# Layer 3's expert FFN: a second activation on ScalarE in place of VectorE's rounding, eight buffers for its results, and weight splits on GpSimd that wait for the normalized x

## What is computed

```python
# x = x + _L3_ffn_ref(_layernorm(x), ...)
shared = silu(x @ sh_up_w + sh_up_b) @ sh_down_w + sh_down_b
scores = softmax(xf @ gate_w.T)
topk_w, topk_i = top_k(scores, 2)
topk_w = topk_w / (topk_w.sum(axis=-1, keepdims=True) + 1e-20)
comb = (one_hot(topk_i, 8) * topk_w[..., None]).sum(axis=1)
h = silu(einsum('nd,edh->neh', xf, up_w) + up_b)
ye = einsum('neh,ehd->ned', h, down_w) + down_b
y = einsum('ned,ne->nd', ye, comb)
return y + shared
```

## Time and profile before

| | us |
|---|---|
| Median of 3 executions | 1869.22 (1867.02 to 1870.14) |
| The profiled execution | 1872.72 |
| its span, from the first to the last instruction | 1870.9 |
| TensorE matmuls busy | 1740.7 (93%) |
| VectorE busy | 1412.7 (76%) |
| ScalarE busy | 1020.7 (55%) |
| GpSimd busy | 640.1 (34%) |

### The profile page before, as it was taken

One profiled execution on the slowest core, in us unless ns is written; L12 is line 12 of the kernel. 1 busy time (PEld: TensorE's weight loads), 2 busy tenths in 40 slices (PEclk: granted clock), 3 DMA queues, 4 the chain that ended last, 5 costly groups with the idle time before them and its releaser, 6 DMA issues. The chain is left out here.

```text
span 1870.9 us, 30938 instructions
## 1 busy us (share of the span) xinstructions
PE 1740.7 (93%) x11311; PEld 1533.4 (82%) x11311; DVE 1412.7 (76%) x3118; ACT 1020.7 (55%) x2239; POOL 640.1 (34%) x906
## 2 busy tenths in 40 slices
PE   6878999999999999999878999999979999999698
PEld 6657899999989999999856888888757788888487
DVE  6467787877878786878676677768877788887786
ACT  3355546555556556555555565656633777776321
POOL 0613030211203030302101455555831666666342
PEclk9989999999999999999999999999989999998799
DMA  5110000000000000000021112110000000000111
GB/s 174 38 48 26 1 7 6 1 12 1 12 1 13 1 12 1 15 1 1 1 91 52 58 56 65 49 68 13 10 1 17 16 18 15 10 10 4 37 54 33
DMA packets 17751, 49.04 MB, mean 26 GB/s; under 512 B 2617, under 2 KB 7362, under 8 KB 15938
## 3 DMA queue, kind: packets, MB, share of 16 engines
q1 hardware_dynamic: 16738, 46.25, 7.6%
q10 hardware_dynamic: 864, 0.83, 0.1%
HBM read 46.15 MB, written 0.92 MB: 25 GB/s over the span
## 5 line engine op out<-in xcount | busy, mean ns | idle before, releaser
L1381 ACT ACTIVATE a_pH<-banks 125x512 fp32r<-125x512 f32 (+1 forms) x384 | 203.9, 544 | 267.6 <-PE banks L195 191.1
L1452 DVE TENSOR_TENSOR a_pL<-banks,a_pH 125x512 fp32r<-125x512 f32 (+1 forms) x384 | 235.4, 623 | 116.6 <-ACT a_pH L1381 114.7
L2011 POOL TENSOR_TENSOR a_prob<-a_prob,a_rinv 112x750 f32<-112x750 f32 x128 | 184.1, 1438 | 196.2 <-DVE a_rinv L2334 196.2
L1433 DVE TENSOR_SCALAR_CACHE_REDUCE a_prob<-banks 128x500 f32<-128x500 f32 x336 | 221.8, 677 | 5.0 <-PE banks L195 4.1
L1225 POOL TENSOR_TENSOR a_head_oH<-a_o,ones 128x256 fp32r<-128x256 f32 (+1 forms) x24 | 16.5, 686 | 605.2 <-DVE a_o L1460 605.2
L1271 PE MATMUL banks<-ident,a_prob 128*125 128x128 f32 x1344 | 201.2, 274 | 6.6 <-ACT a_prob L1366 4.4
L1366 ACT ACTIVATE a_prob<-a_prob,a_nmax 128x1000 f32<-128x1000 f32 x168 | 187.9, 1121 | 32.9 <-DVE a_nmax L1436 32.9
L195 PE MATMUL banks<-a_pH,a_head_vH 125*128 125x256 f32 (+1 forms) x576 | 200.1, 347 | 5.2 <-DVE a_pL L1452 4.3
L1271 PEld LDWEIGHTS banks<-ident,a_prob 128*125 128x125 f32 x1344 | 186.3, 188 | 9.8 <-ACT a_prob L1366 4.9
L195 PE MATMUL banks<-a_pH,a_head_vL 125*128 125x256 f32 (+1 forms) x576 | 173.0, 300 | 0.0
L195 PE MATMUL banks<-a_pL,a_head_vH 125*128 125x256 f32 (+1 forms) x576 | 172.5, 299 | 0.0
(11 more groups left out here) (413 smaller groups left out, 4872.5 us busy)
## 6 DMA issues: line engine op xcount, KB each, us to landing
a_w_out<-in_f_out SPq DMA_DIRECT2D x6, 1024.0 KB, 4.9
a_w_in<-in_f_in SPq DMA_DIRECT2D x12, 512.0 KB, 4.7
f_raw<-in_f_w SPq DMA_DIRECT2D x9, 513.0 KB, 3.5
pair_raw<-in_a_qk SPq DMA_DIRECT2D x16, 256.0 KB, 2.7
pair_raw<-in_a_w SPq DMA_DIRECT2D x8, 384.0 KB, 3.2
a_v<-in_ctx_rows SPq DMA_DIRECT2D x4, 576.0 KB, 7.4
a_kT<-in_f_w SPq DMA_DIRECT2D x2, 1024.0 KB, 5.9
pair_raw<-in_a_wv SPq DMA_DIRECT2D x8, 256.0 KB, 3.4
```

What stands on the lines that cost most here:

```text
L1381: act.activation(pH[:, c % RING, 0:wide], TB[c % 4][0:KB, 0:wide], ACT.Copy).then_inc(t_high, 1)
L1433: dve.tensor_scalar(prob[:, at, c * CHUNK:(c + 1) * CHUNK], SB[c % 3][:, 0:CHUNK], SCALE, None, ALU.mult, ALU.max, accum_out=chunk_max[:, ...
L1452: dve.tensor_tensor(pL[:, c % RING, 0:wide], TB[c % 4][0:KB, 0:wide], pH[:, c % RING, 0:wide].bitcast(F32), ALU.subtract).then_inc(t_done, 1)
L2011: pool.tensor_tensor(both, both, rinv[:, n % RING, :].unsqueeze(2).to_broadcast([SEQ, 2, KEYS]), ALU.mult).then_inc(p_normed, 1)
```

## The change

ScalarE applies the activation twice to each up result. The first writes `hH`, rounded by the output's type, and the second the full value into `hid`. `hid` has eight buffers instead of two. VectorE loses the cast and keeps the subtraction, for which it now waits for both activations. ScalarE gets a wait for the down products of two experts back, which read the `hH` it overwrites, and its wait for the subtraction is now for the one eight steps back. GpSimd waits for the seven normalized tiles before it begins to split the experts' weights.

```diff
@@ layer3_ffn
+    HIDDEN = 8
-        hid = sb("hid", [P, 2, HALF])
+        hid = sb("hid", [P, HIDDEN, HALF])
@@ gpsimd
             router_cut(pool, r, q)
             pool.tensor_copy(comb[:, EXPERTS, :], s.ones[:, 0:TILES]).then_inc(shared_set, 1)
+            pool.wait_ge(ql.normed, TILES)
             cut(0, 0)
             cut(1, 1)
@@ scalar
             def hidden(e, n):
                 act.wait_ge(w_loaded[n], 8 * (e - n) + 16)
+                need(act, y_filled, TILES * (e - 1))
                 for u in range(UPS):
                     step = UPS * e + u
                     act.wait_ge(up_filled, step + 1)
-                    need(act, h_cut, step - 1)
+                    need(act, h_cut, step - HIDDEN + 1)
                     col = raw[n][:, 2 * WIDE + u // 2:2 * WIDE + u // 2 + 1]
-                    act.activation(hid[:, u % 2, :], UB[u][:, 0:HALF], ACT.Silu, bias=col).then_inc(silu_done, 1)
+                    act.activation(hH[n][:, u // 2, HALVES[u % 2]], UB[u][:, 0:HALF], ACT.Silu, bias=col).then_inc(h_high, 1)
+                    act.activation(hid[:, step % HIDDEN, :], UB[u][:, 0:HALF], ACT.Silu, bias=col).then_inc(silu_done, 1)
@@ vector, cut_hidden
                     at = (slice(None), u // 2, HALVES[u % 2])
+                    dve.wait_ge(h_high, step + 1)
                     dve.wait_ge(silu_done, step + 1)
-                    dve.tensor_copy(hH[n][at], hid[:, u % 2, :]).then_inc(h_high, 1)
-                    dve.wait_ge(h_high, step + 1)
-                    dve.tensor_tensor(hL[n][at], hid[:, u % 2, :], hH[n][at].bitcast(F32), ALU.subtract).then_inc(h_cut, 1)
+                    dve.tensor_tensor(hL[n][at], hid[:, step % HIDDEN, :], hH[n][at].bitcast(F32), ALU.subtract).then_inc(h_cut, 1)
```

## The result

| | before | after |
|---|---|---|
| Median, executions on the same chip, us | 1870.24 (1867.02 to 1874.14, 6) | 1855.35 (1852.91 to 1860.02, 6) |
| Ratio of after to before | | 0.9925, 95% interval 0.9912 to 0.9938 |
| The profiled execution, us | 1872.72 | 1855.11 |
| its span | 1870.9 | 1853.3 |

The change saves 14.9 us. The forecast was 14.5 and 1854.7. In the profiled executions the difference is 17.6 us, but only 14.8 of it belong to the change: the last root step (L111), ahead of which no line differs, starts at 1744.89 instead of 1747.65. So from here on I count from the start of L111 in each trace, and totals are compared by medians.

The account below looks back on a forecast made before the run. Bound: TensorE waiting for VectorE's additions in layer 3's FFN, and before it VectorE's norm slowed by GpSimd's splits. Start 8.0 plus loop 6.5 gave 14.5 us off 1869.22: 1854.7, range 1851.5 to 1860.5.

Parts of the forecast that it names:

- T2: Start of expert 2's up products in layer 3's FFN, counted after L111; claimed at 1773.1 in the trace instead of 1781.11.
- The start: Layer 3's FFN up to expert 2's up products: 8.0 us gained, bounds 6.1 and 10.4.
- the loop: Six periods between up(2) and up(8): no stall remains, period 9.90 instead of 10.99, 6.5 us gained.
- The price read from another layer: Layer 2's 7.52 us from L111 to the first up product, taken for layer 3 instead of 14.81: 7.3 us earlier.
- Rival C: Norm in layer 3 stays slow for another reason: only 7.4 us gained, 1861.8; chance 0.08.
- The new collision: Router's steps on VectorE now beside GpSimd's splits: 2.7 us added, bounds 0 and 4.6.
- The second such term: GpSimd's splits for expert 2 beside the last four subtractions of experts 0 and 1: 1.7 us added.
- Rival E: Slower: ScalarE becomes the bound because two activations on one PSUM bank lengthen; 1876 at 2.2 us per pair; chance 0.04.
- The range: Forecast total of the whole kernel, given as 1851.5 to 1860.5 us.
- B: VectorE and GpSimd's exclusion falls badly in the loop: only 2.3 us gained there, 1858.9 in total; chance 0.14.

## Why the prediction was right

By its own steps, in us after L111:

| Step | before | forecast | after |
|---|---|---|---|
| norm of seven tiles | 8.62 | 2.4 | 2.35 |
| up(0) begins | 14.81 | 7.5 | 7.50 |
| router on VectorE ends | 21.11 | 16.55 | 16.07 |
| first down product | 26.21 | 18.85 | 18.39 |
| stall before its fifth tile | 1.24 | 1.5 | 1.34 |
| T2 | 33.46 | 25.45 | 25.13 |
| up(2) to up(8) | 65.91 | 59.4 | 59.40 |

The start gained 8.33 (forecast 8.0) and the loop 6.51 (6.5): 14.84 in the stage.

**The price read from another layer** carried the start. Layer 2 had the order that the change makes, and its 7.52 us came out as 7.50. The run with the wait alone shows the cause: norm 2.35 with no other edit. Rival C is refuted. Not all of the 7.3 us is the norm's: the router's first product comes 6.50 earlier (4.47 after L111 against 10.97), and from there to up(0) it takes 3.03 us instead of 3.84, because before seven of the router's eight products ran at the clock's lower level. The match to 0.02 is partly luck: the same kernel's third run has 8.19, with the clock rising later. It would have changed T2 by 0.27 only.

**The new collision** was rightly seen and slightly oversized: 2.7 us taken, 2.3 measured against the run with the splits moved, well inside the bounds of 0 and 4.6. The splits also ended 12.4 after L111 and not 13.3 as forecast. The second such term, 1.7 for expert 2's splits beside the last four subtractions, was a little too small: they took 4.17 us instead of 2.2, 2.0 more. The two misses leave most of the start's 0.3 us beyond the forecast. The Trainium skill (SBUF — State Buffer, SBUF: two separate sides) calls the port pair that VectorE and GpSimd share an exclusive lock held for a whole instruction, taken by VectorE instructions with two SBUF inputs or in a two-port mode. By that rule, 1.38 and 1.71 beside splits and 0.63 without them are what one expects. By it, the two reductions and the reciprocal, with one input each, should not be lengthened, and they weren't (0.21, 0.21 and 0.20 beside splits and without). The trace agrees with both.

**ScalarE** keeps up, with rounding in the output free (0.63 and 0.63) and a pitch of 0.52 instead of 0.53. Rival E needed 1.9 us per pair and the trace has 1.16; when a third activation raises it to 1.68, TensorE stalls as the rival said.

**The range** has a slip: its upper end is given as 1860.5, where the terms named for it (8.4 off 1869.22) make 1860.8. Nothing hangs on it here.

**The loop** kept no stall, so B is refuted. The first addition was done about 7.34 us after the period's start, where I had 7.5 and TensorE wants it at 7.74. The slack of 0.2 turned out 0.4.

**Where the parts stand.** Alone, the wait is worth 4.9 and the activations 7.6, together 12.5 of the 14.9. The late clock in the profiled execution of the second is worth 2.05 there; if all four of its executions had it, the sum would be 14.5. Only one of them has a trace, so this last point is argued, not shown, and up to 2.4 us between the parts and the whole stay open. The forecast for its start (T2 at 31.0) took the clock as given, a step the prediction had examined only for the path with the wait.

**On transposes and the clock** the rows still go against a rule. The plainest row is that of layer 2: the rise came while TensorE, after standing for 7.63 us, had done nothing but transposes. The busy-time view of the kernel after has the granted clock at 0.50 until 4.60 us after L111 and at 0.78 on average in the next one. It rose at about 5.0, when TensorE had done fourteen transposes and the router's first product, so this row by itself doesn't part the two:

```profile
1744.89:1749.49 4.60, 3.39 (x15) 2.97 (x16) 4.02 (x11) 1.95 (x4) 1.89 (x2) 0.50 0.13 52
1749.49:1750.49 1.00, 1.00 (x5) 0.27 (x4) 0.90 (x2) 0.12 (x1) 1.00 (x2) 0.78 0.00 0
```

Forecasting by the row of layer 2 gave 7.52, measured 7.50. The Trainium skill (TensorE: Matmul & The Clock Gate, Part 4: PE-mode transpose) says that transposes don't count for the clock; by it the prediction made the path 0.9 longer, as an estimate, and this trace doesn't bear that out. The 0.9 was itself low: the router's products start 0.37 us apart at the lower level and 0.20 at the upper, so all eight would cost 1.4. The runs whose up products began at 8.16 and later, with more than half of the eight at the lower level, show that such a delay can happen in part all the same.

## What to carry to other kernels

GpSimd's work in SBUF isn't free because GpSimd is idle: while it runs, whichever chain VectorE is serving pays, here 6.3 us in a norm of 2.35. Such work belongs where VectorE waits or reads PSUM (L184, which reads a bank, took 0.69 beside splits and 0.68 without), and the first question after moving it is what it now runs beside. Buffers between two engines pay nothing while the reader is the slower one; take work off the reader first, and then the buffers are what turns it into time.

## What the runs showed that I had not expected

**The clock's rise isn't fixed by the code ahead of it.** The changed kernel and the wait alone have the same instructions up to the router, and the clock rose 5.0, 4.9, 6.6 and 6.6 us after L111 (after, after again, its third run, the wait alone). The up products then began at 7.50, 7.52, 8.19 and 8.17. Continuous products ahead didn't settle it either. With twelve unread products it rose 1.2 us before L111 in one kernel; in the other, with the splits moved, the busy-time view still shows

```profile
1741.07:1745.90 4.83, 4.82 (x12) 3.78 (x12) 4.35 (x21) 2.21 (x4) 0.55 (x3) 0.50 0.69 222
```

twelve products, 4.82 of 4.83 us busy, and the clock at 0.50; it rose 1.7 us after L111. The same kernel run again had it 0.1 before L111. What decides it stays open. The rise moves this kernel's up products by 0.7 us but T2 by only 0.27 (third run: 25.40 against 25.13), since T2 hangs on VectorE's router. It costs 2 us when it falls on the up products, and it is a floor under what one trace can say about a part.

**A wait in the middle can cost the clock too.** It fell to 0.50 in or just behind waits of 2.88 us (three activations) and 2.59 (eight buffers alone), and what came next ran at half rate. It did not fall in waits of 2.50 and 2.57 (the wait alone, two buffers). What decides between them the runs don't show.

**A small operation can pay as much as a large one, and some don't pay at all.** Beside GpSimd's splits a step on 128 x 7 took 0.97 us instead of 0.17, 0.8 more, about as much as a comparison on 128 x 448 (0.75 and 1.08 more). The loss doesn't go by one's own size; it is of the order of the other engine's instruction (1.04 to 1.55 us). But it falls on some kinds of instruction only. In the router of the kernel after, L709, with two inputs in SBUF, took 0.57 instead of 0.22 (and L698 1.00 instead of 0.22 in the run with the wait alone), while two reductions and a reciprocal ran beside the splits in 0.21, 0.21 and 0.20, as they did before without any.
